# Iteration products on all four corners of the array, values products that give rows, iteration blocks joined, all engines reordered

## The reference: what is computed

```python
V = swapaxes(K, -1, -2) / denom
for _ in range(6):
    KV = K @ V
    V = (0.25 * V) @ (13*I - KV @ (15*I - KV @ (7*I - KV)))
SV = (kernel1 @ V) @ (kernel3 @ values)
```

## Time and profile before

| | us |
|---|---|
| median of 3 runs | 2758.67 |
| the profiled execution | 2757.24 |
| its span | 2755.4 |
| TensorE busy | 2552.7 (93%) |
| VectorE busy | 2122.9 (77%) |
| ScalarE busy | 1334.1 (48%) |
| GpSimd busy | 594.1 (22%) |

### The profile page before, as it was taken

The page is one execution under the profiler, slowest core; times in us unless marked ns, Lnnn a source line. Parts: engine busy times, 40 slices in busy tenths (PEclk is TensorE's granted clock), DMA queues, the critical chain, the costliest instruction groups (busy, mean ns, idle before and its releaser), DMA issues.

```text
span 2755.4 us, 79744 instructions
## 1 busy us (share of the span) xinstructions
PE 2552.7 (93%) x32768; PEld 2080.8 (76%) x32768; DVE 2122.9 (77%) x6528; ACT 1334.1 (48%) x4773; POOL 594.1 (22%) x644
## 2 busy tenths in 40 slices
PE   6689999999999999999999999999999999999885
PEld 4578777777877777787777778787777777777763
DVE  3468878888887888888887888888888878888753
ACT  1345455554545555554555554455555455555431
POOL 0012222222222222222222222222222122222120
PEclk9899999999999999999999999999999999999996
DMA  6000000000000000000000000000000000000000
GB/s 250 6 7 4 8 7 7 7 8 8 4 8 7 7 7 8 8 4 8 6 8 7 8 4 7 8 6 8 7 8 4 8 8 6 8 7 7 4 3 2
DMA packets 29465, 34.71 MB, mean 13 GB/s; under 512 B 3240, under 2 KB 27824, under 8 KB 28464
## 3 DMA queue, kind: packets, MB, share of 16 engines
q1 hardware_dynamic: 29104, 29.62, 3.1%
HBM read 27.51 MB, written 2.10 MB: 11 GB/s over the span
## 4 chain that ended last, share of the span: by engine, by line
PE 70%; DVE 21%; issue 3%; ACT 2%; POOL 2%; POOLq 0%; DVEq 0%
PE ps L527 41%; PE ps L530 13%; PE ps L792 3%; DVE small L1321 3%; PE ps L876 3%; PE ps L922 2%; PE ps L714 2%; PE ps L809 2%; DVE k_alone_q_o L1348 1%; DVE qk_v L1315 1%; PE ps L870 1%; PE ps L936 1%; DVE small L1184 1%; DVE k L1214 1%; POOL probs L1128 1%
## 5 line engine op out<-in xcount | busy, mean ns | idle before, releaser
L1111 POOL TENSOR_TENSOR small<-small,weights 128x1 f32<-128x1 f32 x256 | 141.3, 552 | 1179.2 <-DVE small L1186 1179.2
L1321 DVE TENSOR_REDUCE small<-ps 128x4 f32<-128x512 f32 x384 | 263.3, 686 | 80.1 <-PE ps L876 48.1
L995 ACT COPY ss<-ps 128x288 f32<-128x288 f32 x384 | 154.1, 401 | 325.2 <-PE ps L527 315.4
L1026 ACT ACTIVATE probs<-ps,small 128x128 f32<-128x128 f32 x1024 | 292.4, 372 | 38.0 <-DVE small L1322 35.2
L1328 DVE COPY probsT<-ps 128x512 f32<-128x512 f32 x384 | 263.8, 687 | 45.1 <-PE ps L530 42.1
L1122 POOL TENSOR_SCALAR k_alone_q_o<-qk_v,weights 128x512 f32<-128x512 f32 x128 | 233.2, 1832 | 265.7 <-DVE qk_v L1339 209.9
L530 PE MATMUL ps<-weights,probs 128*128 128x128 f32 x1536 | 250.8, 285 | 14.8 <-POOL probs L1128 11.4
L527 PE MATMUL ps<-wz,ss 64*64 64x72 f32 x6144 | 246.2, 224 | 7.3 <-DVE wz L1278 5.0
L527 PE MATMUL ps<-ey 64*64 64x72 f32 x6144 | 242.8, 227 | 7.5 <-DVE ey L1286 6.9
L527 PEld LDWEIGHTS ps<-wz,ss 64*64 64x64 f32 x6144 | 211.0, 133 | 46.6 <-DVE wz L1278 22.0
L527 PEld LDWEIGHTS ps<-ey 64*64 64x64 f32 x6144 | 211.6, 133 | 42.4 <-issue 32.5
(11 more groups left out here) (199 smaller groups left out, 5558.7 us busy)
## 6 DMA issues: line engine op xcount, KB each, us to landing
weights<-in_wpack SPq DMA_DIRECT2D x1, 5703.5 KB
fc_B<-in_b SPq DMA_DIRECT2D x2, 2048.0 KB, 13.8
fc_A<-in_a SPq DMA_DIRECT2D x2, 2048.0 KB, 23.7
x_in_rows<-in_x SPq DMA_DIRECT2D x32, 64.0 KB, 1.8
x_in_T<-in_xT SPq DMA_DIRECT2D x32, 64.0 KB, 1.8
ctx_T<-in_ctxT SPq DMA_DIRECT2D x32, 64.0 KB, 2.0
ctx_rows<-in_ctx SPq DMA_DIRECT2D x32, 64.0 KB, 1.9
mask_i<-in_mask SPq DMA_DIRECT2D x32, 64.0 KB, 2.0
```

Of the source, the lines that this page charges most:

```text
L995: copy(ss[:, ps], src).then_inc(sem("newton_act", s), 1)
L1026: ins = nc.scalar.activation(probs(s, g)[:, j], bank(s, SCORE_BANK[g], 128 * j, 128), ACT.Exp, bias=sm(s, "nb", 4 * g + j, 1), scale=SC8)
L1111: nc.gpsimd.tensor_tensor(sm(s, out), sm(s, ve), w("mhalf"), ALU.pow).then_inc(sem(done, s), 1)
L1321: link(V.tensor_reduce(sm(s, "mx", 4 * g, 4), bank(s, b).rearrange("p (a b) -> p a b", a=4), AX, ALU.max))
```

## The change

- **Crossing.** The products of half g = 1 go from K rows m to the other output half (`halves[m ^ g]`), so the four products of an (i) use four different 64x64 places. ScalarE takes them back by two copies of 64 partitions each. The last second stage does not cross.
- **Joined blocks.** `n.Sk0` and `n.Sk1` become one TensorE step `n.Sk`, `n.Wk0` and `n.Wk1` one `n.Wk`, each with one semaphore increment at its end; they wait for both halves. `newton_ps` counts 13 a batch instead of 25.
- **VectorE's part of the iteration** makes `wz` in two instructions (64 and 8 columns a pair), the second as 4Y + Ey, and `uy` = Ey + Y afterwards, with a semaphore of its own.
- **Rows instead of columns.** `values`, `n.y0` and `n.o` have 32-column slices of `probsT`, `e3T`, `e1T` as weights and 9 (18 for `n.o`) columns moving: 16, 32 and 32 matmuls instead of 4, 16 and 16. `w9` becomes [128, 8, 2, 9], with zeros outside the head's own half. `tail_turn` and the steps `n.rows` and `r.rows` on TensorE go; ScalarE evicts 72 columns per pair of groups into `orow`; for Nystrom VectorE reads PSUM itself.
- **Values after turns.** `values(0)` moves behind `turn_probs(1)`, `values(2)` behind `turn_probs(3)`, as steps of their own; the same in the 64-wide attention.
- **Scales.** Query weights are multiplied by minus the scale once at the start; maxima become minima and serve directly as the bias, without the multiplication.
- **Padding.** `dropped`, `nT`, `gT`, `b2s` get 128 partitions, cleared at the start.
- **Order.** All `PLACES` and `PERIOD` (79.857 to 87.505, a sorting constant) are new. On TensorE the joined stages now stand with these steps between them: S0, r1.s2 r1.t1 r2.z, W0, r2.y0 r2.out r1.v0, S1, r1.v1 r2.y1 r1.s3, W1, r.ln3 r1.t2 ry.xT, S2, r1.t3 ry.q0 ry.q1, W2, r1.v2 r1.v3 ry.s01, S3, r1.ctxT r1.z r1.y0, W3, r1.out r1.y1 ry.t0, S4, ry.t1, W4, ry.v0 ry.v1 r.ln1, S5, rm.gate rm.h0 ry.s23, W5.

```diff
             for k in range(NEWTON):
-                for g in range(2):
-                    if k:
-                        pe.wait_ge(sem("newton_act", s), at("newton_act", s, 4 * (k - 1) + g + 3))
-                        pe.wait_ge(sem("newton_dve", s), at("newton_dve", s, 4 * (k - 1) + g + 6))
-                    for i, p in enumerate(range(*GROUPS[g])):
-                        for m in halves:
-                            mm = one(PS[s][m, g, PW * i:PW * i + PW], ey[m, p, 0:M], ey[m, p])
-                    mm.then_inc(sem("newton_ps", s), 1)
-                    yield f"n.S{k}{g}"
...
+                last = k == NEWTON - 1
+                if k:
+                    pe.wait_ge(sem("newton_act", s), at("newton_act", s, 4 * k))
+                    pe.wait_ge(sem("newton_dve", s), at("newton_dve", s, 4 * k + 3))
+                for i in range(4):
+                    for g in range(2):
+                        p = 4 * g + i
+                        for m in range(2):
+                            mm = one(PS[s][halves[m ^ g], g, PW * i:PW * i + PW], ey[halves[m], p, 0:M], ey[halves[m], p])
+                mm.then_inc(sem("newton_ps", s), 1)
+                yield f"n.S{k}"
+                pe.wait_ge(sem("newton_dve", s), at("newton_dve", s, 4 * k + 5))
+                a = M if last else 0
+                for i in range(4):
+                    for g in range(2):
+                        p = 4 * g + i
+                        for m in range(2):
+                            mm = one(PS[s][halves[m if last else m ^ g], g, PW * i + a:PW * i + PW], ss[halves[m], p, 0:M],
+                                     wz[halves[m], p, a:PW])
...
-            for h in range(H):
-                g, r, p, m = heads(h)
-                mm = one(PS[s][r, 1, 128 * g:128 * g + 128], w9[m, p], e1T[m, p])
+            for p in range(PAIRS):
+                for r in quarters:
+                    mm = one(PS[s][r, 1, 18 * p:18 * p + 18], e1T[:, p, r], w9[:, p].rearrange("p m e -> p (m e)"))
...
-            tail_turn(s, 1, 1)
-            yield "n.rows"
...
-                for i in range(TG):
-                    mm = one(PS[s][TW * i:TW * i + TW, g // 2, 128 * (g % 2):128 * (g % 2) + 128],
-                             v9[s][:, TJ * g + i], probsT(s, g)[:, i])
+                for i in range(TJ):
+                    for r in quarters:
+                        mm = one(PS[s][r, g // 2, 36 * (g % 2) + 9 * i:36 * (g % 2) + 9 * i + 9], probsT(s, g)[:, i, r],
+                                 v9[s][:, TJ * g + i])
...
+                src, ps = pairs_of(1)
+                for m in range(2):
+                    ins = copy(ss[halves[m], ps], src[halves[1 - m]])
+                ins.then_inc(sem("newton_act", s), 1)
+                yield f"n.S{k}1"
...
-                    link(V.tensor_tensor(Ey, Ey, Y, ALU.add))
-                    a = 0 if k < NEWTON - 1 else M
-                    V.scalar_tensor_tensor(wz[:, ps, a:PW], ey[:, ps, a:PW], 3.0, ss[:, ps, a:PW], ALU.mult, ALU.add
-                                           ).then_inc(sem("newton_dve", s), 1)
+                    if k < NEWTON - 1:
+                        V.scalar_tensor_tensor(wz[:, ps, 0:M], ey[:, ps, 0:M], 3.0, ss[:, ps, 0:M], ALU.mult, ALU.add)
+                    V.scalar_tensor_tensor(wz[:, ps, M:PW], Y, 4.0, Ey, ALU.mult, ALU.add).then_inc(sem("newton_dve", s), 1)
+                    V.tensor_tensor(uy[:, ps], Ey, Y, ALU.add).then_inc(sem("newton_u", s), 1)
...
-            link(V.tensor_reduce(sm(s, "mx", 4 * g, 4), bank(s, b).rearrange("p (a b) -> p a b", a=4), AX, ALU.max))
-            V.tensor_scalar(sm(s, "nb", 4 * g, 4), sm(s, "mx", 4 * g, 4), -scale, None, ALU.mult).then_inc(sem("nb", s), 1)
+            V.tensor_reduce(sm(s, "nb", 4 * (n % 4), 4), bank(s, b).rearrange("p (a b) -> p a b", a=4), AX, ALU.min
+                            ).then_inc(sem("nb", s), 1)
```

More of the change, by code:

```diff
@@ L190, in build @@
         streams = (*lanes, NYS)
-        v9 = [sb(f"v9_{s}", [128, H, TW]) for s in streams]
-        w9 = sb("w9_2", [128, PAIRS, TW])
-        dropped = sb("dropped", [EXPERTS, EXPERTS, 128], BF16)
+        v9 = [sb(f"v9_{s}", [128, H, HD + 1]) for s in streams]
+        w9 = sb("w9_2", [128, PAIRS, 2, HD + 1])
+        dropped = sb("dropped", [128, EXPERTS, 128], BF16)
+        gT = lane("gateT", [128, 128])
+        nT = lane("not_gateT", [128, 128], BF16)
         xin = sb("x_in_rows_2", [128, D])
@@ L268, in link @@
                     dve.wait_ge(steps, count[0])
-                for t in (*v9, w9):
+                for t in v9:
+                    nc.vector.memset(t[:, :, HD:HD + 1], 1.0)
+                link(nc.vector.memset(w9[:], 0.0))
+                for m in range(2):
+                    nc.vector.memset(w9[M * m:M * m + M, :, m, HD:HD + 1], 1.0)
+                for t in (*gT, *nT, dropped):
                     link(nc.vector.memset(t[:], 0.0))
-                    nc.vector.memset(t[:, :, HD:HD + 1], 1.0)
+                nc.vector.memset(b2s[:], 0.0).then_inc(padded, 1)
                 dve.wait_ge(rows_in, 16)
@@ L358, in build @@
         ss = sb("ss_2", [128, PAIRS, PW])
+        uy = sb("u_2", [128, PAIRS, HD])
         wz = sb("wz_2", [128, PAIRS, PW])
         small = [sb(f"small{s}", [128, 192]) for s in streams]
-        oT = [sb(f"oT{s}", [128, TG, 128]) for s in streams]
+        orow = lane("o_rows", [128, H, HD + 1])
         z = [sb(f"z{s}", [128, H, HD]) for s in streams]
@@ L388, in body @@
         o[k] for k in "x xT ctx ctxT mask out W R b2s F1 F2 kaug ident_bf causal_bf dropped w row ident".split())
-    (q1, k1, ql, qlm, klm, v9, w9, e1, p2, e3, e1T, e3T, k2T, ey, ss, wz, xin, xTin) = (
-        o[k] for k in "q1 k1 ql qlm klm v9 w9 e1 p2 e3 e1T e3T k2T ey ss wz xin xTin".split())
+    (q1, k1, ql, qlm, klm, v9, w9, e1, p2, e3, e1T, e3T, k2T, ey, ss, uy, wz, xin, xTin) = (
+        o[k] for k in "q1 k1 ql qlm klm v9 w9 e1 p2 e3 e1T e3T k2T ey ss uy wz xin xTin".split())
     (stored, xs, xTs, x1, x1T, cs, cTs, ms, madd, qk, ka, k8, pp, pT, xbo, cn, xn, cnT, xnT, gT, nT) = (
         o[k] for k in "stored xs xTs x1 x1T cs cTs ms madd qk ka k8 pp pT xbo cn xn cnT xnT gT nT".split())
-    (oT, z, zT, res, PS, sm, over, every) = (o[k] for k in "oT z zT res PS sm over every".split())
+    (orow, z, zT, res, PS, sm, over, every) = (o[k] for k in "orow z zT res PS sm over every".split())
     def bank(s, b, a=0, n=512):
         return PS[s][:, b, a:a + n]
-    def rows_bank(s):
-        return 0
     def out_bank(s):
@@ L446, in body @@
     halves = [slice(M * m, M * m + M) for m in range(2)]
+    quarters = [slice(TW * r, TW * r + TW) for r in range(4)]
     def pairs_of(g):
@@ L530, in turned @@
             return nc.tensor.transpose(dst, src, ident)
-        def tail_turn(s, n_tail, n_oT):
-            pe.wait_ge(sem("oT", s), at("oT", s, n_oT))
-            for g in range(TG):
-                mm = turned(bank(s, rows_bank(s), 128 * g, 128), oT[s][:, g])
-            mm.then_inc(sem("o_rows", s), 1)
         def tail_zT(s, n):
@@ L619, in nystrom @@
             pe.wait_ge(sem("newton_dve", s), at("newton_dve", s, 1))
-            for h in range(H):
-                _, _, p, m = heads(h)
-                mm = one(PS[s][m, 1, 16 * p:16 * p + HD + 1], e3T[:, p, m], v9[s][:, h, 0:HD + 1])
+            for p in range(PAIRS):
+                for r, q in enumerate(quarters):
+                    mm = one(PS[s][q, 1, 16 * p:16 * p + HD + 1], e3T[:, p, q], v9[s][:, 2 * p + r // 2])
             mm.then_inc(sem("n_first_ps", s), 1)
@@ L744, in attention8 @@
             yield f"{a}.s2"
-            values(0)
             turn_probs(1)
             yield f"{a}.t1"
+            values(0)
+            yield f"{a}.v0"
             values(1)
@@ L753, in attention8 @@
             yield f"{a}.t2"
-            values(2)
             turn_probs(3)
             yield f"{a}.t3"
+            values(2)
+            yield f"{a}.v2"
             values(3)
             yield f"{a}.v3"
-            tail_turn(s, n_att, 2 * n_att)
-            yield f"{a}.rows"
             if n_att == 1:
+                pe.wait_ge(sem("o_rows", s), at("o_rows", s, 2))
                 pe.wait_ge(sem("y_norm", s), at("y_norm", s, 1))
@@ L991, in nystrom @@
             for k in range(NEWTON):
[L992 to L1005 removed]
+                act.wait_ge(sem("newton_ps", s), at("newton_ps", s, 2 * k + 1))
+                src, ps = pairs_of(0)
+                copy(ss[:, ps], src).then_inc(sem("newton_act", s), 1)
+                yield f"n.S{k}0"
+                src, ps = pairs_of(1)
+                for m in range(2):
+                    ins = copy(ss[halves[m], ps], src[halves[1 - m]])
+                ins.then_inc(sem("newton_act", s), 1)
+                yield f"n.S{k}1"
+                if k < NEWTON - 1:
+                    act.wait_ge(sem("newton_ps", s), at("newton_ps", s, 2 * k + 2))
+                    act.wait_ge(sem("newton_u", s), at("newton_u", s, 2 * k + 2))
```

(18 more changed lines are left out.)

128 lines of the change are left out of this document (56 added, 72 removed), and 99 rows, old and new, of the table PLACES.

## The result

The changed kernel takes 2719.6 us (median of 4 runs, 2717.5 to 2723.1) against 2757.5 for the kernel before on the same chip: a ratio of 0.986, interval 0.9845 to 0.9879, 1.4% faster. Forecast were 2615 us and 5.2%: the direction and the wide range (2490 to 2810) hold, the size and the forecast's own range (2560 to 2680) don't. The profiled span went from 2755.4 to 2721.4 us.

A forecast was written before the change was run, and what follows sets the result against it. TensorE's work was taken as first bound, then VectorE, then the Nystrom lane. Per batch 34.3 + 37.7 + 3.9 = 75.9 us, 4.5 less; 2757.2 - 32 x 4.5 + 2 - 3 = 2612, stated 2615 us, own range 2560 to 2680, wide 2490 to 2810.

The forecast's parts named there:

- TensorE's work: All TensorE work per batch: falls by 8.5 us, from 77.3 to 68.8.
- The crossing: Iteration stages on four 64x64 places instead of two: 0.62 us instead of 1.15 each, 5.8 us a batch gone.
- Row turns, values, start value, output and shape changes: TensorE outside the iteration, us a batch: turns 1.5, start 0.4, output 0.3, shape changes 1.2 saved; values 0.7 more.
- Joined halves: Between iteration stages both halves end together, so TensorE lacks cover: 3.75 us of shortfalls, say 3.9 with queue waits.
- So TensorE's work is the first bound: Whole kernel: TensorE at 77.3 us of an 80.45 us batch bounds first, VectorE second, the single Nystrom lane third.
- ScalarE's copies: Second half's iteration eviction as two 64-partition copies of 0.4 us: 11 more, 4.4 us; ScalarE under 47, bounding nothing by itself.
- Ends: Start and drain of the run: about 2 us more ahead of the lanes, about 3 us less in the last batches.
- VectorE: VectorE's work per batch: 65.7 to 64.1 us, multiplications after maxima gone (3.3), split product 1.5 and w9 0.2 more.
- (1): Rival: TensorE is handed matmuls one by one at 0.032 us each; 80.2 us of work, 2896 us, slower; 10%.
- (2): Rival: crossed tiles don't run beside straight ones in the iteration; 5.8 us gain missing, 81.7 a batch, 2796 us; 10%.
- (3): Rival: Nystrom lane or VectorE's order gives back more, iterations 5.5 us or more; 2680 to 2757 us; 18%.
- (4): Rival: the joined-half waits don't come, the order leaving enough cover; 71.9 us per batch, 2485 us; 10%.

The follow-up runs named there:

- early_shift128: The change with 32 tiny matmuls ahead of TensorE's list and each lane's next context load issued before the last layer norm wait: 2655.9 us (0.9632).
- shift128: The change with 32 extra tiny matmuls (128 instructions) issued once ahead of TensorE's list: 2693.8 us (0.9774).
- straight: The change with the second half's products not crossed and evicted by one 128-partition copy, stages still joined: 2764.3 us (1.0021).
- onecopy: The change with products crossed but the second half evicted by one 128-partition copy, not crossed back, so iteration numbers differ: 2649.7 us (0.9599).
- before_early: The kernel before with only a lane's next context load issued early: 2734.4 us (0.9914).
- rest_early: rest_only with a lane's next context load issued before the wait for the last layer norm: 2690.6 us (0.9775).
- spread: The change with two TensorE steps, a score product and a turn, moved ahead of iteration 0's first stage: 2747.0 us (0.9961).
- rest_only: The change with the old iteration and old order put back, keeping rows from corners, folded scales and padding: 2723.2 us (0.9874).

## Why the prediction was right in kind and wrong in size

**TensorE's work (right, at full clock).** Forecast 77.3 to 68.8; measured 69.4 in early_shift128 (clock 1.00 in the steady window), 70.0 in shift128 (0.99), 71.2 in the change (0.97). The crossing: from straight to onecopy, which differ in nothing else and have the same clock of 0.98, 74.6 to 69.4, 5.2 of the 5.8. Row turns, values, start value, output and shape changes: 2.7 forecast, 1.9 measured (before_early 77.3, rest_early 75.4).

**Joined halves (size right, names wrong).** Take TensorE's idle time from the first stage of iteration 0 to the last second stage, as a mean of 24 batches from 400 us on. Before it is 0.3 us; in the change 5.2, of which 1.4 are gaps without a wait. So 3.8 for the 3.9 forecast, and 3.9 and 4.1 in shift128 and early_shift128. But the profile puts only 0.6 of it down to ey and wz. The steps that I had counted as cover between the stages wait themselves: 1.4 for GpSimd's probabilities, 1.2 of it ahead of the second stage of iteration 4, where I had forecast the worst (1.55), and 0.7 for VectorE's x_norm ahead of the first stage of iteration 2, where I had 0.75. Outside that stretch TensorE idles 3.1 us, before 2.9, as I had left it.

**"So TensorE's work is the first bound" (the step that failed).** I counted TensorE's new work at full clock and added the joined halves to its present idling. The supply of instructions stood in the sum at nothing, without a reason, though the change needs a quarter more of them. The runs show in its place 1.4 us a batch of gaps and, at a clock of 0.97, 71.2 of work for 68.8. These two are the 3.5 us by which the period misses (79.42 for 75.9). They can't be had back by the shift alone, since a second limit lies just beneath: the lane's turn from store to load to projections. The shift brings 26 us and the early load another 38; that is 64 of the 105 us by which the change missed the forecast. But of the 38 some 22 are paid by the kernel before as well, and so were in the times from which I forecast: against the forecast the two account for about 42.

**ScalarE's copies (price right).** 0.393 and 0.405 for 0.4. Its work is 453.97/800 x 79.42 = 45.1 us, and it never was full; but its list is a fixed one, a longer eviction moves all exponentials behind it, and the third operation costs 69.9 us in all (onecopy). "Bounds nothing by itself" is true and hides this. Most of it was in my sum, though: with 0.4 less at each joined eviction the shortfalls are 1.95 for 3.75, that is 58 us less. So for onecopy I should have said some 2557, and it takes 2650 (2622 with the shift). With the shift the iteration idles 2.95 us for the 2.1 that this gives, and the projections wait 0.9 for the load. The agreement of 2622 with 2615 is therefore no proof of my sum.

**Ends.** I multiplied by 32. There are some 29 full periods; in the first three (start to v,e3T, then two periods) the change takes 228 us for 203, and 193 for 216 after the last. That is 3 us more where I had 1 less, and 3 x 4.5 us of gain that isn't there: 17 us of the miss. The same settles what is left in early_shift128. Its profiled execution took 2646.6 us, 35 more than the 2612 of the sum: 13 for these three periods, 10 for the ends (235 for 203, and 192 for 216), and 11 for 29 periods that are 4.1 us shorter and not 4.5.

**VectorE (right).** 634.27/800 x 79.42 = 63.0 for the 64.1.

**The rivals.** (1) fell: 32 records in 0.66 us, 64 in 0.67 to 0.74, where it wanted 0.032 each. The Trainium skill, "TensorE: Matmul & The Clock Gate", section "Wait — 56ns, not 53.3ns?", has matmuls start no closer than about 25 ns; here 32 take 0.66 us (21 ns each) and 64 take 0.67, so the trace disagrees for tiles side by side. (2) fell: the four places run together, 0.66 where the two took 1.15. (3) named the time, 2680 to 2757, and its "5.5 us or more" an iteration came true. Its part on "half-partition copies and rest steps between them in the queues" is shown by onecopy; "the lane itself sets" is not: from the second stage group of ey to the last, the starts of the change (1018.37, 1024.48, 1030.63, 1036.32, 1041.63) and of early_shift128 (1007.53, 1013.64, 1019.79, 1025.48, 1030.79) are the same distances apart, 6.11, 6.15, 5.69 and 5.31, and the period differs by 3 us. (4) fell.

So 2680 to 2757 was right partly by luck: the gaps and the clock behind them, which no rival names, are what the period misses by.

**Open.** That a gap is the wait for one 16 KB piece is read from the records (the packet in front of it, its drift through the list, the effect of the shift and of spread, and none of the shift in the kernel before), not isolated: no kernel had its instructions all there. Why a load takes longer beside such a packet isn't shown. Why the joined stages without crossing cost 41 us against rest_only (straight against rest_only) is not taken apart: the order changed with them. The early load was run neither without the shift nor together with onecopy's edit, so how the 64 us divide between the two, and what ScalarE's third operation costs with both away, isn't known.

## What to carry to other kernels

When TensorE gets several per cent less work in a kernel where it is 96% busy, list every other resource that is a few per cent below it, the turn from store to load to first product of a lane and the instructions themselves included, for these can set the gain, and not the removed work. An operation on an engine at 50% is not free if the engine runs a fixed list: count what stands behind it there. Idle time that a profile puts down to nothing is worth placing: within a group it was the instructions, ahead of the first product of a batch it was a load. And try a load's issue point in the old kernel too: 22 us were to be had there without any of the change.

## What the hardware showed unexpectedly

TensorE stopped 1.7 us within a group that waited for nothing, next to one instruction packet of 16 KB and some 1.16 us, and then ran at 0.51 of its clock for 3.5 us; 16 or 32 more matmuls at the start took away 16 or 26 us of 2720. A load of 64 KB that lands after 1.9 us otherwise took 2.5 to 3.6 us in 25 batches of shift128, in all of them beside an instruction packet. Matmuls on four crossed 64x64 places start about 21 ns apart (32 in 0.66 us), on 128x32 places about 10 ns (64 in 0.67). A ScalarE copy of 64 partitions takes as long as one of 128 (393 and 398 ns for 288 columns).
